# Edge counting in 128 groups of 256 edges with a 24-target span, against 64 groups of 512 with 40

## The chip, the cores and the metric

The kernel runs on one core of a Trainium2 chip. A core has a tensor engine (PE), a vector engine (DVE), a scalar engine (ACT), GpSimd (POOL) and a sync engine (SP), each with its own instruction stream; they wait for each other on semaphores. The metric is device time in microseconds (us) of one execution, and the median of several runs is compared.

## The reference, cut to what matters

Four graph layers, each followed by a residual and a normalisation, work on 1024 nodes of 512 features and 32768 edges, sorted by target. Everything the layers need of the graph comes from one table: how many edges lead from source s to target t.

```
x, src, dst: 1024x512 float32, 32768 int32, 32768 int32 (dst is sorted)
edge_index = stack([src, dst])
layer 0: adj.set(1) both ways, + eye, degree-normalised, adj @ (x @ weight) + bias
layer 1: three graph convolutions: segment_sum(xw[src] * norm, dst) + b
layer 2: q, k, v; attention masked by adj = zeros(N, N).at[src, dst].set(1)
layer 3: two graph convolutions, a relu between them
after each: x = layernorm(x + layer)
```

## The kernel before

The whole kernel is one block with a program written by hand for each engine. It has a counting stage and then the layers. The counting stage builds `count`, a table of 1024 sources by 1024 targets in SBUF, out of the sorted edge list.

The edges are cut into G groups of GE = CPG * 128. In each group the targets lie close together, and a window of WIN targets from the group's smallest one takes them all, if the group's span is under WIN. If the widest group's span is not, the stage is run again for the next WIN targets (a "round"; `rounds` is computed on the chip from the widest span). For one group there are CPG chunks of 128 edges, one edge per partition. Each chunk takes two one-hot matrices: `hot_lo`, 128 wide, the source modulo 128, and `hot_key`, KEYS = 8 * WIN wide, a key made of the source's block of 128 and the target's place in the window. One bf16 matmul per chunk multiplies the two (L479), and the CPG chunks are summed in one PSUM bank. DVE then adds the bank to the window of `count` (L950).

The engines share this work as follows.

- DVE makes every `hot_key` (L936) and the `hot_lo` of the first BY_DVE chunks (L934) of group g+1, and then waits for the matmuls of group g and adds its window (L950). The target address comes from a register; eight registers are loaded at once, for BODY = 8 groups (L941).
- ACT makes the other `hot_lo` in two steps, since it has no comparison: the absolute difference into `apart`, one instruction per chunk (L788), then, after a wait for them, one relu over all of them into `hot_lo` (L792). It may start group g when the matmuls of group g-2 are done, since `hot_lo` and the PSUM banks 0 and 1 are used in turn. Behind that stand the copies of folding results from PSUM (L782 and neighbours), 512 columns each.
- PE waits for the add of group g-2 and for each one-hot, does the CPG matmuls, and then does its share of other work that doesn't need the graph: the "folding". That is a list of 48 units of 4 pieces each (transposes of x and of weights L419 and L423, products L431, L454, L458, L461, bias rows L436 and L449). A credit decides how many pieces stand behind a group: it grows by SHARE per group, and a piece costs 1024 of it for a 512-column product, 128 for a transpose and 256 for a piece of the small bias unit.

```
        for g in range(-1, G):
            m = n
            while credit > 0 and m < 4 * (NU - 1):
                credit -= weight_of(m)
                m += 1
            pieces[g] = (n, m)
            n = m
            credit = min(credit, 0) + SHARE
```

What is left of the list follows behind the last group; then come the transposes of the links (L521), the last unit, and layer 0 (L544). Each 1024-credit piece is one fp32 product, which the trace records as two matmuls.

POOL adds a bias to `xs` in eight instructions (L352) as soon as the small bias unit is out. That falls into the counting stage.

Of the kernel before, what the change touches and what calls it, by code (L numbers as in the profile page):

```python
# [28 lines left out]
NEG = -1000000.0  # L29
EXACT = 4096  # L30
FAR = 8192.0
CPG = 4
WIN = 40
BY_DVE = 2
EARLY = 24 * 128
SHARE = 1450
BODY = 8
HALF = 4

# [1 line left out]
def gnn_kernel(nc, x, src, dst, w0, b0, w1, b1, w2, b2, w3, b3, wq, bq, wk, bk, wv, bv, v1, c1, v2, c2, out):  # L41
# [3 lines left out]
    FB = D // P  # L45
    G = E // (CPG * P)
    GE = CPG * P
    ROUNDS = (N + WIN - 1) // WIN
    KEYS = NB * WIN
    SCALE = float(D) ** -0.5  # L50
    assert D == 512 and NB == 2 * HALF and G % BODY == 0 and KEYS <= 512 and G <= P

    with ExitStack() as ctx:
        place = [(nc.sbuf_base + 63) // 64 * 64]

        def region(size):

            start = place[0]
            place[0] += (size + 31) // 32 * 32
            assert place[0] <= nc.sbuf_usable_end  # L60
            return start

        def at(name, start, shape, dt):
            return nc.alloc_sbuf_tensor_at(name, shape, dt, offset=start)

        def sb(name, shape, dt):
            size = {F32: 4, F32R: 4, I32: 4, BF16: 2, I16: 2, U16: 2}[dt]
            for n in shape[1:]:
                size *= n
            return at(name, region(size), shape, dt)  # L70
# [5 lines left out]
        adj = sb("adj", [P, NB, N], F32R)  # L76
        count = sb("count", [P, NB, N + WIN], U16)
        xs = sb("xs", [P, NB, D], F32)
# [38 lines left out]
        key_rows = at("key_rows", r3 + 2 * W + 8192, [G, 3, GE], F32)  # L117
        keyed = at("keyed", r3 + 2 * W, [P, 3, CPG * G], F32)
        apart = at("apart", r3 + 2 * W + 8192, [P, 2, CPG - BY_DVE, P], BF16)
        link = at("link", r3 + 2 * W, [P, NB, N], BF16)  # L120
# [8 lines left out]
        r4 = region(W)  # L129
        hot_lo = at("hot_lo", r4, [P, 2 * CPG, P], BF16)  # L130
        hot_key = at("hot_key", r4 + 2 * CPG * P * 2, [P, 2 * CPG, KEYS], BF16)
        wv_sb = at("wv_sb", r4, [P, FB, D], F32)
# [125 lines left out]
        for g in range(-1, G):  # L258
# [5 lines left out]
            n = m  # L264
            credit = min(credit, 0) + SHARE
        ALONG = n
# [56 lines left out]
        def _(pool):  # L323
            chain = [0]

            def then(ins):
# [8 lines left out]
            nc.gpsimd.tensor_copy(identb[:], ident[:])  # L335
            nc.gpsimd.iota(span_at[:], pattern=[[WIN, ROUNDS]], base=0, channel_multiplier=0,
                           allow_small_or_imprecise_dtypes=True)
# [68 lines left out]
        def _(pe):  # L406
# [78 lines left out]
            for g in range(G):  # L485
                pe.wait_ge(win_added, g + 1)
                for c in range(CPG):
                    pe.wait_ge(hot_set, CPG * g + c + 1)
                    if c == BY_DVE:
                        pe.wait_ge(act_hot_set, g + 1)  # L490
# [7 lines left out]
            with pe.If(rounds > 1):  # L498
                with pe.Fori(1, rounds) as r:
                    with pe.Fori(0, G // BODY) as q:  # L500
                        for n in range(BODY):
                            pe.wait_ge(win_added, r * G + q * BODY + (n + 1))
                            for c in range(CPG):
                                pe.wait_ge(hot_set, (r * G + q * BODY) * CPG + (n * CPG + c + 1))
                                if c == BY_DVE:
                                    pe.wait_ge(act_hot_set, r * G + q * BODY + (n + 1))
# [254 lines left out]
        def _(act):  # L761
# [23 lines left out]
            def low_one_hots(g, slot, before):  # L785

                for c in range(BY_DVE, CPG):
                    ins = nc.scalar.activation(apart[:, slot, c - BY_DVE, :], col_lo[:], ACT.Abs, scale=-1.0,  # L788
                                               bias=edge_key[:, 0, bass.ds(g + c * G, 1)])
                ins.then_inc(apart_set, 1)  # L790
                act.wait_ge(apart_set, before + 1)
                nc.scalar.activation(hot_lo[:, slot * CPG + BY_DVE:(slot + 1) * CPG, :], apart[:, slot], ACT.Relu,  # L792
                                     scale=-1.0, bias=ones[:, 0:1]).then_inc(act_hot_set, 1)
# [95 lines left out]
        def _(dve):  # L889
# [20 lines left out]
            V.tensor_copy(key_rows[:, 0, :], bits[:, 0, :])  # L910
            V.tensor_scalar(key_rows[:, 1, :], bits[:, 1, :], float(WIN), None, ALU.mult)
            V.tensor_scalar(key_rows[:, 2, :], edge_rows[:, 0, :], group_lim[:, 0:1], None,
# [33 lines left out]
            def add_window(at_dst, seen, slot):  # L946

                dve.wait_ge(win_summed, seen + 1)
                dve.wait_ge(win_added, seen + 2)
                V.tensor_tensor(count[:, :, bass.ds(at_dst, WIN)],  # L950
                                bank[:, slot, 0:KEYS].rearrange("p (h d) -> p h d", h=NB),
# [251 lines left out]
```

## Time and profile before

| | us |
|---|---|
| median of 3 runs | 622.41 |
| lowest and highest run | 619.67, 624.84 |
| span of the profiled execution, first to last instruction | 620.4 |
| counting stage, first one-hot (ACT) to the end of the last window add | 14.4 to 144.7 |
| PE busy in the span | 593.8 |
| DVE busy in the span | 300.0 |
| ACT busy in the span | 180.1 |

The profiled execution has no time of its own in the list beside its span; the span lies between the lowest and the median run. Busy times are shares of engines, and an engine that is not on the chain that ends last may be idle at no cost. A matmul's duration in the trace includes its way through the array, so the step from one start to the next is the better measure of what it costs.

### The profile page before, as it was taken

The page shows a single profiled execution, that of the slowest core. Times are in us where ns is not written, and L with a number is a line of the kernel's source. Part 1 is how long each engine was busy: PE and PEld are TensorE (multiplying, and loading weights), DVE is VectorE, ACT ScalarE, POOL GpSimd, SP SyncE. Part 2 cuts the span into 40 slices and gives each one's busy share as a digit, 9 for nine tenths or more (in the row PEclk, how much of TensorE's full clock was granted, in tenths as well). Part 3 has the DMA queues.
Part 4 walks back from the last instruction along what each step waited for, and adds up shares of the span by engine and source line. Part 5 has one row for each costly group of instructions (what it writes and reads, how often), then busy time and mean ns, then how long its engine had stood idle before and what let it go on. Part 6 is the DMA issues. An engine that isn't in the chain of part 4 may idle for free.

```text
span 620.4 us, 6559 instructions
## 1 busy us (share of the span) xinstructions
PE 593.8 (96%) x2153; PEld 351.9 (57%) x2153; DVE 300.0 (48%) x818; ACT 180.1 (29%) x363; POOL 108.8 (18%) x121
## 2 busy tenths in 40 slices
PE   3997899999997999999999999999999999999996
PEld 3554365454665557888874544444444478548742
DVE  6989977895734710343459110323333550251055
ACT  2787467783610230121100301211112311221100
POOL 3003200000822530000026000222222161000012
PEclk9999798999998999999999999999999999999999
DMA  8500003002000000000004000000000000000012
GB/s 297 195 1 1 0 1 137 0 2 69 2 0 2 0 3 0 1 0 1 0 6 147 0 1 0 0 1 0 1 0 0 2 1 1 0 0 1 0 52 85
DMA packets 7903, 15.65 MB, mean 25 GB/s; under 512 B 432, under 2 KB 448, under 8 KB 7872
## 3 DMA queue, kind: packets, MB, share of 16 engines
q1 hardware_dynamic: 7872, 15.21, 7.0%
q8 instruction: 22, 0.36, 0.2%
q14 instruction: 9, 0.07, 0.0%
HBM read 13.12 MB, written 2.10 MB: 25 GB/s over the span
## 4 chain that ended last, share of the span: by engine, by line
PE 90%; DVE 4%; ACT 2%; issue 2%; DMA 0%; POOL 0%; POOLq 0%; SPq 0%; DVEq 0%; ACTq 0%
PE bank L544 17%; PE bank L597 17%; PE bank L561 10%; PE bank L706 9%; PE bank L726 9%; PE bank L479 6%; PE bank L694 4%; PE bank L454 4%; PE bank L458 2%; PE bank L461 2%; PE bank L431 2%; PE bank L449 2%; PE bank L716 1%; PE bank L624 1%; DVE hot_key L936 1%
## 5 line engine op out<-in xcount | busy, mean ns | idle before, releaser
L370 POOL TENSOR_TENSOR rstd<-veps,mhalf 128x1 f32<-128x1 f32 x32 | 23.6, 737 | 299.4 <-DVE veps L1009 292.4
L936 DVE TENSOR_SCALAR hot_key<-col_key,keyed 128x320 bf16<-128x320 int16 x256 | 70.5, 317 | 0.0
L706 PE MATMUL bank<-xt,tt 128*128 128x512 f32 x128 | 56.1, 592 | 0.0
L726 PE MATMUL bank<-vv,probt 128*128 128x512 f32 x128 | 56.1, 592 | 0.0
L597 PE MATMUL bank<-v_sb,gt 128*128 128x512 f32 x128 | 55.3, 592 | 0.0
L479 PE MATMUL bank<-hot_key,hot_lo 128*128 128x320 bf16 x256 | 48.5, 309 | 4.6 <-DVE hot_key L936 4.5
L479 PEld LDWEIGHTS bank<-hot_key,hot_lo 128*128 128x128 bf16 x256 | 25.7, 100 | 47.2 <-issue 21.8
L788 ACT ACTIVATE apart<-col_lo,edge_key 128x128 bf16<-128x128 int16 x128 | 44.4, 396 | 26.8 <-PE bank L479 26.6
L561 PE MATMUL bank<-adj,y_hi 128*128 128x512 f32 x128 | 51.8, 405 | 0.0
L544 PE MATMUL bank<-ya_hi,adj 128*128 128x512 f32 x128 | 50.9, 398 | 0.0
L544 PE MATMUL bank<-ya_lo,adj 128*128 128x512 f32 x128 | 50.5, 395 | 0.0
L561 PE MATMUL bank<-adj,y_lo 128*128 128x512 f32 x128 | 50.2, 392 | 0.0
L1016 DVE SCALAR_TENSOR_TENSOR xs<-bank,dinv,xs 128x512 f32<-128x512 f32 x24 | 17.9, 747 | 53.9 <-PE bank L597 38.4
L597 PEld LDWEIGHTS bank<-v_sb,gt 128*128 128x128 f32 x128 | 24.3, 190 | 29.8 <-issue 29.2
L726 PEld LDWEIGHTS bank<-vv,probt 128*128 128x128 f32 x128 | 24.2, 190 | 29.6 <-issue 29.6
L706 PEld LDWEIGHTS bank<-xt,tt 128*128 128x128 f32 x128 | 23.9, 190 | 27.7 <-issue 27.7
L950 DVE TENSOR_TENSOR count<-bank,count 128x320 f32 x64 | 31.2, 487 | 14.6 <-PE bank L479 14.5
L1116 DVE SCALAR_TENSOR_TENSOR score<-bank,rr,mask 128x1024 f32<-128x1024 f32 x8 | 10.3, 1284 | 55.5 <-PE bank L706 55.5
L934 DVE TENSOR_SCALAR hot_lo<-col_lo,edge_key 128x128 bf16<-128x128 int16 x128 | 34.4, 268 | 3.4 <-issue 3.3
L454 PE MATMUL bank<-w_sb,x0t 128*128 128x512 f32 x64 | 31.7, 597 | 2.0 <-ACT x0t L769 1.7
L792 ACT ACTIVATE hot_lo<-apart,ones 128x256 bf16<-128x256 bf16 x64 | 32.5, 508 | 2.1
L544 PE MATMUL bank<-ya_hi,sym 128*128 128x512 f32 x64 | 28.0, 438 | 4.5 <-DVE flags L1057 3.7
(172 smaller groups left out, 894.5 us busy)
## 6 DMA issues: line engine op xcount, KB each, us to landing
w_sb<-in_L_gnn_W_dram SPq DMA_DIRECT2D x3, 1024.0 KB, 7.7
xs<-in_x_dram SPq DMA_DIRECT2D x2, 1024.0 KB, 8.2
v_sb<-in_L_gnn_W_dram SPq DMA_DIRECT2D x2, 1024.0 KB, 6.8
out_dram<-xs SPq DMA_DIRECT2D x8, 256.0 KB, 2.0
w_sb<-in_L_gnn_weight_dram SPq DMA_DIRECT2D x1, 1024.0 KB, 8.5
wq_sb<-in_L_gnn_Wq_dram SPq DMA_DIRECT2D x1, 1024.0 KB, 12.5
wk_sb<-in_L_gnn_Wk_dram SPq DMA_DIRECT2D x1, 1024.0 KB, 13.9
wv_sb<-in_L_gnn_Wv_dram SPq DMA_DIRECT2D x1, 1024.0 KB, 6.4
```

The source lines that it names most:

```text
L454: mm = pe.matmul(to, x0t[:, k, rows], w0_sb[:, k, :], start=first, stop=last)
L479: return pe.matmul(bank[:, at_bank, 0:KEYS], hot_lo[:, at_hot, :], hot_key[:, at_hot, :], start=c == 0, stop=c == CPG - 1)
L544: mm = pe.matmul(to, m[:, k, j * P:(j + 1) * P], y[part][:, k, :], start=k == 0 and part == 0 and m is mat, stop=k == NB - 1 and part == 1 ...
L561: mm = pe.matmul(to, y[part][:, k, f * P:(f + 1) * P], m[:, k, half], start=k == 0 and part == 0 and m is mat, stop=k == NB - 1 and part = ...
L597: mm = pe.matmul(bank[:, HALF * (s % 2) + b, :], g[:, k, j * P:(j + 1) * P], w[:, k, :], start=k == 0, stop=k == FB - 1)
L706: mm = pe.matmul(bank[:, 2 * (i % 2) + c, :], tt[:, k, i * P:(i + 1) * P], xt[:, k, c * D:(c + 1) * D], start=k == 0, stop=k == FB - 1)
L726: mm = pe.matmul(bank[:, 6 + i % 2, :], probt[:, i % 2, j, :], vv[:, j, :], start=j == 0, stop=j == NB - 1)
L788: ins = nc.scalar.activation(apart[:, slot, c - BY_DVE, :], col_lo[:], ACT.Abs, scale=-1.0, bias=edge_key[:, 0, bass.ds(g + c * G, 1)])
L792: nc.scalar.activation(hot_lo[:, slot * CPG + BY_DVE:(slot + 1) * CPG, :], apart[:, slot], ACT.Relu, scale=-1.0, bias=ones[:, 0:1]).then_i ...
L934: V.tensor_scalar(hot_lo[:, slot * CPG + c, :], col_lo[:], edge_key[:, 0, bass.ds(g + c * G, 1)], None, ALU.is_equal)
L936: V.tensor_scalar(hot_key[:, slot * CPG + c, :], col_key[:], keyed[:, 0, bass.ds(g + c * G, 1)], None, ALU.is_equal).then_inc(hot_set, 1)
L950: V.tensor_tensor(count[:, :, bass.ds(at_dst, WIN)], bank[:, slot, 0:KEYS].rearrange("p (h d) -> p h d", h=NB), count[:, :, bass.ds(at_dst ...
```

## The change

Four numbers change, and through them the sizes and counts. G goes from 64 to 128, GE from 512 to 256, KEYS from 320 to 192. A group now has two chunks, one low one-hot by DVE and one by ACT. The credit per group is half. No other line changes.

```diff
-CPG = 4
-WIN = 40
-BY_DVE = 2
+CPG = 2
+WIN = 24
+BY_DVE = 1
 EARLY = 24 * 128
-SHARE = 1450
+SHARE = 725
 BODY = 8
 HALF = 4
```

On PE, in the first part of the counting stage, the matmuls of one or more groups (L479) stand between products of the folding (L454: the rows of x by the weight of layer 0). Before:

```order
L479 MATMUL bank<-hot_key,hot_lo 128x320 x4
L454 MATMUL bank<-w_sb,x0t 128x512
L479 MATMUL bank<-hot_key,hot_lo 128x320 x4
L454 MATMUL bank<-w_sb,x0t 128x512 x2
L479 MATMUL bank<-hot_key,hot_lo 128x320 x4
```

After the change:

```order
L479 MATMUL bank<-hot_key,hot_lo 128x192 x2
L454 MATMUL bank<-w_sb,x0t 128x512
L479 MATMUL bank<-hot_key,hot_lo 128x192 x4
L454 MATMUL bank<-w_sb,x0t 128x512
L479 MATMUL bank<-hot_key,hot_lo 128x192 x2
L454 MATMUL bank<-w_sb,x0t 128x512
L479 MATMUL bank<-hot_key,hot_lo 128x192 x2
```

A group is four matmuls before and two after; where "x4" stands after the change, two groups follow each other with no folding between them. There were one or two folding products behind each group, and there is now one or none.

On ACT, at the start of the stage, before:

```order
L788 ACTIVATE apart<-col_lo,edge_key 128x128 x2
L792 ACTIVATE hot_lo<-apart,ones 128x256
L788 ACTIVATE apart<-col_lo,edge_key 128x128 x2
L792 ACTIVATE hot_lo<-apart,ones 128x256
L782 COPY xw<-bank 128x512
```

After the change:

```order
L788 ACTIVATE apart<-col_lo,edge_key 128x128
L792 ACTIVATE hot_lo<-apart,ones 128x128
L788 ACTIVATE apart<-col_lo,edge_key 128x128
L792 ACTIVATE hot_lo<-apart,ones 128x128
L782 COPY xw<-bank 128x512
```

Each group's pair on ACT has become one difference and one relu of half the width, and there are twice as many groups.

On DVE, one group of the loop before (with the register instructions between the operations):

```order
L934 TENSOR_SCALAR hot_lo<-col_lo,edge_key 128x128
L936 REGISTER_ALU
L936 TENSOR_SCALAR hot_key<-col_key,keyed 128x320
L934 ISA
L934 TENSOR_SCALAR hot_lo<-col_lo,edge_key 128x128
L936 REGISTER_ALU
L936 TENSOR_SCALAR hot_key<-col_key,keyed 128x320
L936 ISA
L936 TENSOR_SCALAR hot_key<-col_key,keyed 128x320
L936 ISA
L936 TENSOR_SCALAR hot_key<-col_key,keyed 128x320
```

After the change, with the add that follows:

```order
L934 TENSOR_SCALAR hot_lo<-col_lo,edge_key 128x128
L936 REGISTER_ALU
L936 TENSOR_SCALAR hot_key<-col_key,keyed 128x192
L936 ISA
L936 TENSOR_SCALAR hot_key<-col_key,keyed 128x192
L948 ISA
L949 REGISTER_ALU
L950 ISA
L950 TENSOR_TENSOR count<-bank,count 128x8x24
```

A window add now stands behind three one-hot instructions where it stood behind six.

## Rows read from the trace of the kernel before

**Rows 1.** The page: the span, and PE's busy tenths in 40 slices.
```profile
span 620.4 us, 6559 instructions
PE   3997899999997999999999999999999999999996
```

**Rows 2.** The chain that ended last, in order of time (start, us, what).
```profile
60.23 3.71 DVE hot_key L936 x3
...
144.00 7.74 PE bank L461 x18
152.40 1.51 PE bank L521 x24
```

**Rows 3.** The timeline, 22.0 to 26.2 (start, us, engine, line, operation, idle before).
```profile
22.04 0.71 PE L479 MATMUL bank<-hot_key,hot_lo 128*128 128x320 bf16 x4
...
22.59 1.02 PE L454 MATMUL bank<-w_sb,x0t 128*128 128x512 f32 x2
22.79 0.69 ACT L788 ACTIVATE apart<-col_lo,edge_key 128x128 bf16<-128x128 int16 x2 [0.82 <-PE bank L479]
22.98 0.49 DVE L950 TENSOR_TENSOR count<-bank,count 128x320 f32 x1 [0.43 <-PE bank L479]
...
23.39 0.24 DVE L934 TENSOR_SCALAR hot_lo<-col_lo,edge_key 128x128 bf16<-128x128 int16 x1
23.45 0.71 PE L479 MATMUL bank<-hot_key,hot_lo 128*128 128x320 bf16 x4
...
23.51 0.51 ACT L792 ACTIVATE hot_lo<-apart,ones 128x256 bf16<-128x256 bf16 x1
23.55 0.30 DVE L936 TENSOR_SCALAR hot_key<-col_key,keyed 128x320 bf16<-128x320 int16 x1
23.76 0.25 DVE L934 TENSOR_SCALAR hot_lo<-col_lo,edge_key 128x128 bf16<-128x128 int16 x1
...
23.99 1.88 PE L454 MATMUL bank<-w_sb,x0t 128*128 128x512 f32 x4
...
24.56 0.48 DVE L950 TENSOR_TENSOR count<-bank,count 128x320 f32 x1
...
24.91 0.51 ACT L792 ACTIVATE hot_lo<-apart,ones 128x256 bf16<-128x256 bf16 x1
24.96 0.24 DVE L934 TENSOR_SCALAR hot_lo<-col_lo,edge_key 128x128 bf16<-128x128 int16 x1
...
25.33 0.57 ACT L782 COPY xw<-bank 128x512 f32<-128x512 f32 x1
...
25.70 0.71 PE L479 MATMUL bank<-hot_key,hot_lo 128*128 128x320 bf16 x4
```

**Rows 4.** Waits, 15 to 145 (us in total, times, longest).
```profile
ACT apart L788 <- PE bank L479: 26.6, 33, 4.9
...
DVE count L950 <- PE bank L479: 14.5, 21, 4.8
...
PE bank L479 <- DVE hot_key L936: 4.5, 5, 2.1
```

**Rows 5.** One line each: ACT's differences, DVE's register loads (min/median/max ns).
```profile
L788 ACT ACTIVATE apart<-col_lo,edge_key x128: 384/400/433, 14.4 to 140.9; 128x128 bf16<-128x128 int16 x128
```

```profile
L941 DVEq TENSOR_LOAD <-base_at x8: 594/599/633, 15.5 to 130.2; - x8
```

**Rows 6.** The timeline: a stretch of transposes, and DVE behind a register load.
```profile
30.74 0.26 DVE L934 TENSOR_SCALAR hot_lo<-col_lo,edge_key 128x128 bf16<-128x128 int16 x1 [0.46 <-issue]
...
48.50 1.47 PE L423 MATMUL bank<-ident,wq_sb 128*128 128x128 f32 x12
```

**Rows 7.** Windows of 3 us (busy time and count by engine, PE's granted clock).
```profile
51.00:54.00 3.00, 2.35 (x17) 1.83 (x17) 3.00 (x15) 2.97 (x9) 0.00 (x0) 1.00 0.02 5
...
60.00:63.00 3.00, 0.53 (x2) 0.19 (x2) 3.00 (x4) 0.00 (x0) 3.00 (x4) 1.00 0.00 0
63.00:66.00 3.00, 2.09 (x4) 0.58 (x3) 3.00 (x4) 1.20 (x3) 3.00 (x3) 0.55 0.00 0
66.00:69.00 3.00, 2.62 (x7) 1.15 (x7) 3.00 (x13) 1.13 (x3) 0.28 (x1) 0.50 0.00 0
```

## The prediction

> **What bounds the kernel now.** I read the page first. PE is busy nine tenths or more in most slices, the counting stage included [rows 1], so the question is whether PE itself or its partners set the pace there. The chain of waits answers it for the end of the stage: PE runs through its leftover folding (7.74 us) and goes straight on to the link transposes [rows 2]. The leftover folding hides the last window add and what DVE does to the links, so the rest of the kernel starts when PE's list is done, and the stage is worth what PE spends in it, work and waits. The list behind it isn't touched, nor is anything after 152 us.
>
> Then I read the timeline group by group, from one start to the next, since matmul durations overlap [rows 3]. PE starts a group at 22.04, 23.45 and 25.70. The first lasts 1.41 us: 0.54 for the four counting matmuls (23.45 to 23.99) and 0.86 for one product of the folding. The second has two products and lasts 2.25. Neither has a gap: with the sum 0.54 + 0.86 n the group is over when PE's own work is. DVE needs less for a group: its adds start at 22.98 and 24.56, a period of 1.58 us, and it is DVE that waits for PE (14.5 us in all); ACT waits for PE as well (26.6 us); PE waits for one-hots only 4.5 us [rows 4]. These 4.5 us are in one place, where POOL adds its biases and each DVE one-hot takes over 1.2 us (three in 3.71) [rows 2]. So PE binds, and its partners have slack.
>
> **Does the narrower window suffice?** From the reference's inputs, the widest of the 128 groups spans 17 targets, less than 24. There is one round, as before (widest of the 64: 32, under 40).
>
> **PE's counting matmuls (a gain).** 64 groups x 0.54 = 34.6 us. Four matmuls of 320 columns in 0.54 is 0.135 each; by columns, 192 take 0.081. 128 groups x 0.16 = 20.5 us. Gain 14.1 us at the clock of the rows. The folding is the same list, and because the credit per edge is the same, it ends at the same place of the list: no change, and the 7.74 us leftover stays.
>
> **What DVE needs per group.** From starts [rows 3]: `hot_lo` 0.16 (23.39 to 23.55), a 320-wide `hot_key` 0.21 (23.55 to 23.76), the 320-wide add 0.40 (24.56 to 24.96). That is 2 x 0.16 + 4 x 0.21 + 0.40 = 1.56. Widths 128 and 320 differ by 0.05, so a 192-wide key takes about 0.175. The add has no row at another width. Ends: 0.24, if all of it goes with the columns, and 0.40, if none does. I take 0.27 (0.13 us less for 128 columns fewer), nearer the first, because the one-hots show a fixed part of some 0.12 and no more. Then 0.16 + 2 x 0.175 + 0.27 = 0.78 per group of half the size: the same time per edge, hence no gain on DVE. The registers are loaded every eight groups, so 16 times and not 8; a load takes 0.6 [rows 5] and shows as 0.46 of idle time before the next one-hot [rows 6], that is 0.06 more per group: 0.84.
>
> **What ACT needs per group.** The two differences take 0.69, the relu starts 0.03 after them (22.79 to 23.51), and it holds the engine for 0.42 (24.91 to 25.33) [rows 3]; a single difference takes 0.40 [rows 5]. That is 1.14 per group, 73 us in all. After the change one difference stands before its wait: 0.40 + 0.04, and nothing overlaps it. A 128-wide relu holds the engine for about 0.30: no row shows it, but the second of two 128-wide differences adds 0.29 (0.69 less 0.40), and the 256-wide relu's 0.42 is the upper end. So 0.74 per group, 128 x 0.74 = 95 us: 22 us more for the same edges. Some 42 copies at 0.50 (0.57 less the overlap of 0.09) stand between: 21 us, or 0.16 per group.
>
> A rule of the Trainium skill bears on both engines: "VectorE: DVE Perf Modes", section on the TRN2 errata, states a fixed cost per instruction, 58 cycles plus the width over the mode's factor on VectorE and 224 cycles on ScalarE. By it a 192-wide one-hot would be about 0.11 us and DVE's group near 0.65; the rows have 0.16 for the narrowest one, so the row is used. If the rule's figure held in this loop, the forecast would be about 3 us lower.
>
> **The hand-offs (a loss).** PE needs 0.16 + 0.86 n, with n one or none. Averaged over the credit (725 of 1024) that is 0.77, beside 0.84 for DVE and 0.90 for ACT. What were 1.75, 1.62 and 1.5, with PE the slowest, are now nearly equal, with PE the fastest; PE must wait. Where it does follows from the order of instructions. Of the 127 groups with a successor, 75 have one product behind them, 32 have none, 20 have transposes or the small bias unit.
>
> - One product: PE has 1.02 us of its own, more than its partners. Wait about 0.03. 75 x 0.03 = 2 us; ends 0 and 0.2 each (15 us), the latter if PE meets a partner that is behind.
> - None: PE has only 0.16, and the two buffers carry it one group ahead at most. Over a typical run of three groups (product, product, none) PE has 2 x 1.02 + 0.16 = 2.20, DVE 2.5, ACT 2.5 (3 x 0.74 and half a copy). So the empty group can't take less than about 0.47. If it waits for a full period of DVE, it takes 0.78. The add can start 0.4 us after the last matmul's issue (the matmuls of 22.04 end at 22.75, the add starts at 22.98) [rows 3], and that delay now stands in a group half as long. I take 0.65, in the middle: wait 0.49, 32 x 0.49 = 16 us; ends 10 and 20.
> - Transposes: six or so behind a group, at 0.12 [rows 6], are 0.16 + 0.72 = 0.88 for PE; in nearly each such group a 512-wide copy falls due on ACT, which then needs 0.74 + 0.50 = 1.24. The copies lag a little and are partly caught up. Wait 0.2 each, 4 us; ends 0 and 7.
>
> Sum of waits 22 us, less the gain of 14: **+8 us**. With all low ends it is -4, with all high ends +28, which would need every partner late in every group. POOL's stretch stays as it is: its eight instructions block DVE's one-hots for the same time, and the one-hots per edge are as many as before (six for 512 edges, three for 256), so PE loses the same there. DVE's setup ahead of the loop gets shorter in the 64-partition steps, but PE waits there for x, not for it: nothing.
>
> **The clock.** PE's granted clock is 1.00 up to 63 us and then 0.55 and 0.50, 1.2 GHz, after PE had been busy for 0.53 of 3 us in POOL's stretch; with 2.35 of 3 it stayed at 1.00, 2.4 GHz [rows 7]. After the change PE would be busy some 83% of the stage, in gaps under 0.6 us, nearer to the second row. So I count no further loss, and keep one as a rival.
>
> **Rivals.**
>
> 1. *The engines' slack suffices*: each group costs what the slowest engine needs and no more; the empty groups take 0.47, the transposes nothing. For it: PE, DVE and ACT wait for each other through two buffers and the groups without a product are evenly spread. Against: three engines with nearly the same load rarely mesh. Sum -14 + 10 + 2 to 4: about 0, 622 us.
> 2. *PE stays the slowest*: the one-hot instructions turn out shorter at half width (a relu near 0.2, an add near 0.2), and DVE and ACT fall under 0.7 per group. The waits shrink to some 5 us in all. Then the columns saved are gained: 622.4 - 9 = 613 us. It decides at a partner's load of 0.77 per group, PE's own. Against it: the differences' 0.40 and the keys' 0.16 are at 128 columns already and can't shrink.
> 3. *The clock falls as well*: PE's micro-gaps bring it to 1.2 GHz in further stretches. A product then takes 1.72 and the partners have to wait. With two or three more such stretches of 7 us as in 63 to 70 [rows 7], each costing 3 to 4 us, +16 to +18 in all: 639 us. For it: half as much cover at each gap, and the transposes' stretches, in which PE waits most. Against it: the row at 2.35 of 3 us. The Trainium skill has this as a rule, in "TensorE: Matmul & The Clock Gate", section "A second HAM failure mode: psum-queue depth-cycling": frequent micro-idles between groups of matmuls that cycle through banks make the clock oscillate. No row of before shows that.
> 4. *A second round* would add a whole stage, over 100 us. The inputs exclude it.
>
> **How the numbers follow.** The sum is made against the span of 620.4; the median is 2.0 above it, and the difference is carried over: 622.4 + 8 = 630.5 (own range 626 to 636). Chances: forecast 0.50, rival 1 0.20, rival 2 0.08, rival 3 0.22. The runs shown spread over 5 us, so 1%, 6.2 us, is about what a measurement can tell from no change. Slower by over 1% (above 628.6): 0.42 of the forecast's 0.50 and rival 3, 0.64. Within 1%: the rest of the forecast and nearly all of rival 1, 0.27. Faster: rival 2 and a little of rival 1, 0.09. A range from 620 to 642 leaves out rival 2, the lower part of rival 1 and the far end of rival 3, less than 0.2 together.
>
> **What the profile after would show.** PE's steps with one product near 1.02 to 1.05, the empty ones near 0.65: under 0.5 speaks for rival 1 or 2, over 0.8 for a dearer hand-off. The steps from DVE add to one-hot, 0.27, and from ACT's relu to the next instruction, 0.30, are the two sizes not seen. The last window add should end near 152.5 and not at 144.7, the leftover folding follow it unchanged, and PE's wait for one-hots of both kinds rise from 4.5 to over 20 us. A granted clock under 1.00 outside the two stretches of before would be rival 3. The prediction is wrong above all if ACT or DVE run their narrow instructions faster than their 128-wide ones of before.

## The result, and the profile after

The changed kernel takes 635.14 us at the median (634.49 to 636.41, 4 runs), the kernel before 622.41. The ratio is 1.0224, with a 95% interval of 1.0193 to 1.0255: slower by 12.7 us by the medians and by 13.9 us by the ratio. The profiled execution has a span of 633.9 us, 13.5 more than before.

The page, span and PE by slices, to be read beside [rows 1]:

```profile
span 633.9 us, 6994 instructions
...
PE   4987689989999799999999999999999999999996
```

PE's digits have fallen to 6 to 9 in the first quarter, where almost all were 9. The first link transpose on the chain of waits shows where the time went. It stood at 152.40 [rows 2]:

```profile
157.47 6.29 PE bank L461 x14
163.78 0.59 ACT wfold L782
164.42 1.51 PE bank L521 x24
```

So 12.0 of the 13.5 us are in the counting stage. Most of the rest, 1.2 us, is at the first feature transposes (L624), 1.75 us on the chain before and 2.97 after: the 1.2 GHz stretch at PE's wait there lasts 6.8 us, where it lasted 3.4. The same place has either length in the runs below. In the counting stage the difference goes the other way: the 1.2 GHz stretch behind the bias unit lasts 3.4 us in this trace (98.6 to 102.0) and 6.8 in that of before (90.6 to 97.4). If such a stretch costs half its length, which is an estimate, that is up to 1.7 us in favour of the changed kernel, and at equal clock the stage has grown by up to 13.7 us.

Now the groups, in the timeline of the changed kernel at the place of [rows 3]:

```profile
21.81 0.36 DVE L950 TENSOR_TENSOR count<-bank,count 128x192 f32 x1 [0.27 <-PE bank L479]
22.05 0.40 ACT L792 ACTIVATE hot_lo<-apart,ones 128x128 bf16<-128x128 bf16 x1
22.09 0.24 DVE L934 TENSOR_SCALAR hot_lo<-col_lo,edge_key 128x128 bf16<-128x128 int16 x1
22.25 0.44 DVE L936 TENSOR_SCALAR hot_key<-col_key,keyed 128x192 bf16<-128x192 int16 x2
22.36 0.39 ACT L788 ACTIVATE apart<-col_lo,edge_key 128x128 bf16<-128x128 int16 x1
22.61 0.35 DVE L950 TENSOR_TENSOR count<-bank,count 128x192 f32 x1
22.70 0.33 PE L479 MATMUL bank<-hot_key,hot_lo 128*128 128x192 bf16 x2
...
22.90 1.10 PE L454 MATMUL bank<-w_sb,x0t 128*128 128x512 f32 x2
...
23.72 0.25 DVE L934 TENSOR_SCALAR hot_lo<-col_lo,edge_key 128x128 bf16<-128x128 int16 x1 [0.76 <-issue]
...
24.30 0.37 PE L479 MATMUL bank<-hot_key,hot_lo 128*128 128x192 bf16 x2 [0.29 <-DVE hot_key L936]
```

The add holds DVE for 0.28 (21.81 to 22.09), the relu holds ACT for 0.31 (22.05 to 22.36): the sizes that no row of before showed are as estimated. Then DVE loads eight registers, is idle for 0.76, its next one-hots come late, and PE, whose product began at 22.90 and has some 0.9 us of work in it, starts the next group only at 24.30: this group lasts 1.60 us. The waits of the stage, to be read beside [rows 4]:

```profile
ACT apart L788 <- PE bank L479: 19.0, 32, 2.2
PE bank L479 <- DVE hot_key L936: 14.6, 22, 2.2
...
DVE hot_lo L934 <- issue: 12.4, 16, 0.9
DVE count L950 <- PE bank L479: 12.0, 36, 2.1
PE bank L479 <- ACT hot_lo L792: 2.7, 5, 1.0
```

PE's wait for DVE has gone from 4.5 to 14.6 us, and DVE's idle time behind its 16 loads is 12.4, 0.77 each. Of the low one-hots of ACT PE waits only 2.7.

From the starts of each group's first matmul in the trace, and for the groups called quiet without POOL's stretch and the slow-clock stretch behind the bias unit:

| groups of the changed kernel | count (quiet) | forecast, us | mean | median |
|---|---|---|---|---|
| one product behind | 75 (65) | 1.05 | 1.22 | 1.18 |
| none behind | 32 (29) | 0.65 | 0.46 | 0.35 |

In the kernel before, the quiet groups with one product all took 1.40 and those with two 2.26 (median), PE's own work.

Two things in the trace say where the excess stands. The 12 quiet groups in whose course DVE loads its registers, so that the next group's one-hots come late, take 1.66 with a product and 1.15 without; the others take 1.15 and 0.38. And a product itself has become dearer: its second matmul starts 0.43 us after the first in the trace of before, and 0.46 or 0.50 in the changed kernel, the longer step in 15 of the 18 products just behind a wait of PE and in 22 of the 54 others. Over these 72, all outside the slow-clock stretches, it is 3.8 us. Why a product costs more behind a small group isn't shown.

### The profile page after: what moved, and what is told of

Its sections match the earlier page's. It is cut to its first block, busy times and chain, and to the rows that moved or that the text cites. A ratio compares the mean times of both kernels' runs of the same rounds, so it can differ in the third digit from the quotient of the medians.

```text
span 633.9 us, 6994 instructions
## 1 busy us (share of the span) xinstructions
PE 594.7 (94%) x2147; PEld 345.0 (54%) x2147; DVE 304.6 (48%) x882; ACT 201.2 (32%) x427; POOL 108.7 (17%) x121
## 4 chain that ended last, share of the span: by engine, by line
PE 79%; DVE 9%; issue 5%; ACT 4%; DVEq 2%; POOL 0%; DMA 0%; POOLq 0%; SPq 0%
PE bank L544 17%; PE bank L597 17%; PE bank L561 9%; PE bank L706 9%; PE bank L726 9%; PE bank L694 4%; DVE hot_key L936 3%; PE bank L454 3%; PE bank L479 2%; PE bank L461 2%; PE bank L449 2%; DVE hot_lo L934 2%; PE bank L624 1%; ACT hot_lo L792 1%; PE bank L716 1%
## 5 line engine op out<-in xcount | busy, mean ns | idle before, releaser
L479 PEld LDWEIGHTS bank<-hot_key,hot_lo 128*128 128x128 bf16 x256 | 25.0, 99 | 80.3 <-issue 51.3
L479 PE MATMUL bank<-hot_key,hot_lo 128*128 128x192 bf16 x256 | 46.1, 248 | 18.2 <-DVE hot_key L936 14.6
L936 DVE TENSOR_SCALAR hot_key<-col_key,keyed 128x192 bf16<-128x192 int16 x256 | 61.9, 284 | 0.1
L788 ACT ACTIVATE apart<-col_lo,edge_key 128x128 bf16<-128x128 int16 x128 | 50.7, 396 | 20.3 <-PE bank L479 19.0
L792 ACT ACTIVATE hot_lo<-apart,ones 128x128 bf16<-128x128 bf16 x128 | 51.4, 402 | 4.1
L950 DVE TENSOR_TENSOR count<-bank,count 128x192 f32 x128 | 45.5, 356 | 13.7 <-PE bank L479 12.0
L934 DVE TENSOR_SCALAR hot_lo<-col_lo,edge_key 128x128 bf16<-128x128 int16 x128 | 33.5, 262 | 12.4 <-issue 12.4
L454 PE MATMUL bank<-w_sb,x0t 128*128 128x512 f32 x64 | 34.6, 622 | 2.3 <-ACT x0t L769 2.3
```

The lines of the kernel that those rows point to most:

```text
L454: mm = pe.matmul(to, x0t[:, k, rows], w0_sb[:, k, :], start=first, stop=last)
L479: return pe.matmul(bank[:, at_bank, 0:KEYS], hot_lo[:, at_hot, :], hot_key[:, at_hot, :], start=c == 0, stop=c == CPG - 1)
L934: V.tensor_scalar(hot_lo[:, slot * CPG + c, :], col_lo[:], edge_key[:, 0, bass.ds(g + c * G, 1)], None, ALU.is_equal)
L936: V.tensor_scalar(hot_key[:, slot * CPG + c, :], col_key[:], keyed[:, 0, bass.ds(g + c * G, 1)], None, ALU.is_equal).then_inc(hot_set, 1)
L950: V.tensor_tensor(count[:, :, bass.ds(at_dst, WIN)], bank[:, slot, 0:KEYS].rearrange("p (h d) -> p h d", h=NB), count[:, :, bass.ds(at_dst ...
```

## The experiments

Each ratio is to runs of the kernel before on the same chip; the changed kernel is at 1.0224 on this scale, and 0.01 is 6.2 us. These intervals are 0.0013 to 0.003 to either side. The runs of the kernel before aren't all alike, even on one chip: 620.6 us and less where the granted clock was 0.986 or more, 621.8 and more where it was 0.984 or less. So a ratio also carries which of the two a chip's runs happened to show, and differences under some 2 us between runs on different chips aren't sure. "Links start" is the first L521 in the trace: 152.4 before, 164.4 after.

**Deeper buffers (e1_deep).** Four buffers of one-hots, four PSUM banks, DVE two groups ahead, and ACT's wait for a free buffer set back likewise. The main lines of the edit:

```diff
-        hot_lo = at("hot_lo", r4, [P, 2 * CPG, P], BF16)
+        hot_lo = at("hot_lo", r4, [P, SLOTS * CPG, P], BF16)
-                pe.wait_ge(win_added, g + 1)
+                pe.wait_ge(win_added, max(g + 3 - SLOTS, 2))
-                        one_hots(q * BODY + (n + 1), (n + 1) % 2)
+                        one_hots(q * BODY + (n + AHEAD), (n + AHEAD) % SLOTS)
```

> The changed kernel (635.1 us) with four buffers of one-hots and four PSUM banks where there are two, and DVE making its one-hots two groups ahead. No work is changed. Theory H (hand-offs: the groups cost more than the busiest engine needs because two buffers tie PE, ACT and DVE together): quiet groups fall from a mean near 0.98 us towards ACT's own 0.90, so 8 to 10 us come back, 625 to 627. Rival L (load: DVE or ACT alone sets the pace, its instructions plus the register loads are what a group costs): no more than 2 us come back, 633 to 635.

Measured: 626.92 us, ratio 1.0105 (1.0082 to 1.0128), links start at 155.6. 7.4 us of 13.9 come back by the ratio, 8.2 by the medians, and the links start 8.9 earlier with 1.2 GHz stretches of the same length. So H holds for the greater part, and L is out. The empty groups take 0.165 at the median and those with a product 1.05, PE's own; by the mean it is 0.29 and 1.21, so some groups still wait. What PE still waits for:

```profile
PE bank L481 <- DVE hot_key L938: 9.5, 16, 2.3
PE bank L481 <- ACT hot_lo L794: 5.2, 11, 1.0
```

**Sixteen registers at a load (e2_body16).**

```diff
-BODY = 8
+BODY = 16
```

> The changed kernel with the registers of the window targets loaded for 16 groups at once, so 8 loads and not 16. In the changed kernel DVE sat idle 12.4 us behind the 16 loads, 0.77 each. If the load sits on the path each time (theory: the register loads are a dearer term of the sum than the 0.46 taken from before), 8 x 0.6 to 0.8 = 5 to 6 us come back: 629 to 630. Rival: PE or ACT is behind anyway when the load comes, and at most 2 us come back, 633 or more.

Measured: 632.55 us, ratio 1.0198 (1.0174 to 1.0222). That is 1.6 us at the centre, within the intervals, and near the rival's figure; but the rival's reason isn't shown by it, since the edit didn't do what I meant. Half as many loads take nearly twice as long each, and DVE sits idle behind the 8 for 10.1 us where it was 12.4 behind 16. The line of the loads in this run (median 1101 ns; 599 for eight registers [rows 5]):

```profile
L941 DVEq TENSOR_LOAD <-base_at x8: 1096/1101/1133, 14.8 to 138.2; - x8
```

From these two durations the price is 0.06 us per register and 0.1 per load, an estimate, so it goes with the number of groups.

**ACT's difference ahead (e3_actpipe).** The main lines of the edit:

```diff
+            low_apart(0, 0)
             for g in range(G):
-                if g >= 2:
-                    act.wait_ge(win_summed, g - 1)
-                low_one_hots(g, g % 2, g)
+                if g + 1 < G:
+                    if g >= 3:
+                        act.wait_ge(act_hot_set, g - 2)
+                    low_apart(g + 1, (g + 1) % 4)
+                if g >= 2:
+                    act.wait_ge(win_summed, g - 1)
+                low_relu(g % 2, g % 4, g)
```

> The changed kernel with ACT's difference for group g+1 issued ahead of the relu of group g (four buffers for the differences), so that the relu's wait for its difference is covered. Occupancy per group by the rows of after: 0.74 falls to about 0.29 + 0.31 = 0.60, and the way from a freed buffer to the finished low one-hot from 0.84 to 0.41. If ACT's pair is what delays the groups (theory A), 6 to 12 us come back, 623 to 629. If DVE's one-hots and its loads are (rival D), under 2 us: 633 or more.

Measured: 631.71 us, ratio 1.0176 (1.0151 to 1.0201), links start at 162.0: 3.0 us. It lies between the two: ACT isn't the main delay while there are two buffers, but it isn't nothing. (In the traces the links start 2.4 us earlier.)

**The grouping alone (e4_win40).**

```diff
-WIN = 24
+WIN = 40
```

> One part of the change alone: 128 groups of 256, with the old window of 40 targets (320 columns). Per group PE then needs 0.27 for its matmuls and not 0.16, DVE 0.06 to 0.07 more for two wider keys and 0.13 more for the add. Theory: with partners as the pace, DVE's 0.20 more per group counts in full, 128 x 0.2 = 25 us: 660. Rival (PE's columns count, since it is PE that is on the chain): 128 x 0.107 = 14 us, 649. Against the kernel before it is the grouping alone, so the narrower window is worth the difference of this run to 635.

Measured: 642.68 us, ratio 1.0364 (1.0338 to 1.0391), links start at 172.1. The grouping alone costs 22.7 us, and the narrower window gives 8.7 back. Both figures for the latter were too high, and neither theory holds in full. The quiet groups with a product keep their 1.22 and only the empty ones grow, from 0.46 to 0.73: a group with a product had room for DVE's longer instructions, and an empty one hadn't, as I read it; no run separates the two.

**Deeper buffers and ACT ahead (e5_deep_act).** The two edits together.

> Both earlier edits together on the changed kernel: four buffers and banks, and ACT's differences issued ahead. With the buffers alone (ratio 1.0105 to the kernel before) ACT still keeps PE waiting 5.2 us, at the copies. If those waits are what is left besides DVE's loads, 3 to 5 us more come back: ratio 1.003 to 1.006. If DVE's own pace (its instructions and the register loads, some 0.86 us a group) is the limit now, less than 1.5 us: ratio 1.008 to 1.011.

Measured: 621.4 us, ratio 0.998 (0.9966 to 0.9994), links start at 150.1. With both edits the kernel is level with the one before: the whole loss has come back, 15.2 us by the ratio and 13.7 by the medians. How much of it the second edit adds to the first is less sure, since the two ran on different chips: 7.8 us by the ratios, 5.5 by the medians. In the trace the links start 5.5 us earlier than in e1_deep, of which up to 1.7 are the clock's: the stretch at 1.2 GHz behind POOL's adds lasts 3.4 us here and 6.8 in e1_deep. That leaves 3.8, inside the 3 to 5 expected. PE's wait for ACT's one-hots has fallen from 5.2 to 1.0 us, which is of that size:

```profile
PE bank L481 <- ACT hot_lo L797: 1.0, 2, 0.5
```

That ACT's pair was worth more with four buffers than its 3 us with two isn't shown.

**No register loads (e6_noload).** The output is not the reference's: all windows go to eight fixed places, and the add takes a fixed address with them. The step from an add to the next one-hot stays 0.27 us, so the address form changes nothing.

```diff
-                _, values = nc.values_load_multi_w_load_instructions(
-                    base_at[0:1, bass.ds(g, BODY)], engines=[mybir.EngineType.DVE], min_val=0, max_val=N,
-                    skip_runtime_bounds_check_because="the table's entries are clamped to [0, N] when it is written")
+                values = [n * P for n in range(BODY)]
-                V.tensor_tensor(count[:, :, bass.ds(at_dst, WIN)],
+                V.tensor_tensor(count[:, :, at_dst:at_dst + WIN],
```

> The changed kernel without the register loads: the windows go to eight fixed places of the count table, so the targets of the edges are left out of the placing; every count, add, one-hot and matmul stays. In the trace of the changed kernel a group at nearly every eighth place lasts 0.6 to 1.2 us longer. Theory: each of the 16 loads (0.60 us for 8 registers, over 1.1 for 16) falls on the path; without them 10 to 13 us come back, 622 to 625 where the changed kernel has 635. Rival: PE would wait for the hand-offs instead, and 4 us or less come back (631 or more).

Measured: 629.72 us, ratio 1.0116 (1.0098 to 1.0135), links start at 159.3. The loads are on the path: 6.7 us come back by the ratio (5.4 by the medians), between the theory's 10 to 13 and the rival's 4 at most. DVE now waits for PE in 47 groups and not 36, for 19.1 us and not 12.0, so part of the time taken away comes back as that wait.

```profile
DVE count L948 <- PE bank L479: 19.1, 47, 3.2
```

**A narrower window alone (e7_win34),** in the kernel before.

```diff
-WIN = 40
+WIN = 34
```

> The kernel before, 64 groups of 512, with a window of 34 targets (the widest group spans 32), 272 columns for 320. If PE's columns set the pace there (steps of 1.40 and 2.26 without a gap), 256 x 48 columns at 2.4 GHz = 5.1 us come off: ratio 0.992. If DVE or ACT would be next at once, less than half of it: 0.996 or more.

Measured: 616.9 us, ratio 0.9914 (0.9895 to 0.9932), links start at 146.1. The whole 5 us came. (In the traces the links start 6.3 us earlier, up to 1.7 of it from a shorter 1.2 GHz stretch behind the bias unit.) The timeline of PE shows a step of 1.32 with one product (1.40 before) and 2.18 with two (2.25), with no gap:

```profile
21.78 0.63 PE L479 MATMUL bank<-hot_key,hot_lo 128*128 128x272 bf16 x4
22.25 1.02 PE L454 MATMUL bank<-w_sb,x0t 128*128 128x512 f32 x2
23.10 0.63 PE L479 MATMUL bank<-hot_key,hot_lo 128*128 128x272 bf16 x4
23.57 1.88 PE L454 MATMUL bank<-w_sb,x0t 128*128 128x512 f32 x4
25.28 0.63 PE L479 MATMUL bank<-hot_key,hot_lo 128*128 128x272 bf16 x4
```

This version beats both kernels with one number, and is the best here that computes the reference.

**The partners' pace by itself (e8_nofold).**

```diff
-SHARE = 725
+SHARE = 0
```

> The changed kernel with no folding between the groups (a share of 0): all of it runs behind the last group. Not meant as an improvement; it shows what a group costs when PE has only its two matmuls. By DVE's rows (0.78 of instructions and a load of 0.6 to 0.76 every eight groups) 0.86 to 0.88 us per group; ACT alone would give 0.74. If the hand-off chain through two buffers is longer than that, 1.0 us or more. PE would be at 1.2 GHz here.

Measured: 695.36 us in its one run, PE at 1.2 GHz for 122.9 us. Only the group's period is of use. Its timeline, a group and the next behind a load:

```profile
65.33 0.48 PE L479 MATMUL bank<-hot_key,hot_lo 128*128 128x192 bf16 x2 [0.31 <-DVE hot_key L936]
...
66.12 0.48 PE L479 MATMUL bank<-hot_key,hot_lo 128*128 128x192 bf16 x2 [0.31 <-DVE hot_key L936]
...
67.27 0.25 DVE L934 TENSOR_SCALAR hot_lo<-col_lo,edge_key 128x128 bf16<-128x128 int16 x1 [0.85 <-issue]
...
67.85 0.48 PE L479 MATMUL bank<-hot_key,hot_lo 128*128 128x192 bf16 x2 [1.25 <-DVE hot_key L936]
...
68.73 0.48 PE L479 MATMUL bank<-hot_key,hot_lo 128*128 128x192 bf16 x2 [0.40 <-DVE hot_key L936]
```

A group takes 0.79 (median 0.786), which is DVE's 0.78 of instructions; the hand-offs add nothing to it. Behind a load it takes 1.73. The 127 steps sum up to 115.6 us, 0.91 each: (115.6 - 127 x 0.786) / 16 = 0.99 us per load on average, twice what I had counted.

**The share undone (e9_share1450).**

```diff
-SHARE = 725
+SHARE = 1450
```

> The changed kernel with one part undone: the folding share per group is 1450 again, so the folding is used up after some 65 of the 128 groups. Those have one or two products (0.16 + 1.22 on average = 1.38 us, PE's own), the 62 or so behind them have none and go at DVE's pace, 0.91 (the run without folding). Sum: 65 x 1.38 + 62 x 0.91 = 146 us where the changed kernel's groups took 141, and no folding is left to cover the last window add and the links, but 6.3 us of it no longer stands behind the stage either. Theory (pace of DVE where PE has nothing): near the changed kernel, -2 to +4 us: ratio 1.02 to 1.03. If the halved share were itself what costs the time, this would be back near the kernel before: 1.01 or less.

Measured: 658.32 us, ratio 1.0588 (1.0559 to 1.0618). The halved share isn't what costs the time; with the old one it would have been far worse. The time lies 18 us over the upper end of my own figure. The 58 empty groups do take 0.90 each, as in the run without folding. But the sum for the others left out POOL's stretch, the transposes and the slow clock (112 us and not 90), and PE's clock falls to 1.2 GHz once the folding is used up. PE was busy for 1.95 of 3 us and then 1.04 of 3 before that (126 to 132), and in it:

```profile
130.00:150.00 20.00, 10.34 (x44) 4.53 (x44) 17.94 (x89) 16.56 (x44) 0.00 (x0) 0.57 0.00 1
150.00:170.00 20.00, 10.23 (x44) 4.36 (x42) 17.43 (x87) 16.49 (x44) 0.00 (x0) 0.50 0.00 0
```

The clock stays at 0.50 for 54.6 us in this trace, into the first 24 link transposes, which take 4.25 us where they took 1.51.

**Everything ahead, window of 18 (e10_deep_act_win18).**

```diff
-WIN = 24
+WIN = 18
```

> The changed kernel with four buffers, ACT's differences ahead, and a window of 18 targets (the widest group spans 17), 144 columns for 192. With the buffers PE is mostly without a gap (steps 1.05 and 0.165 at the median), so 256 x 48 columns = 5.1 us of PE and 128 x 0.05 of DVE's add come off. If PE or DVE sets the pace either way: ratio 0.990 to 0.992 where the same with 24 had 0.998. If DVE's one-hots and register loads are what is left, which hardly shrink: 0.995 to 0.998.

Measured: 619.55 us, ratio 0.996 (0.9945 to 0.9975). Within the second figure: 256 x 48 columns less bring 1 us and not the 5 of e7_win34. PE is no longer what paces the stage here. The shortest group with a product has itself fallen by only 0.02, from 1.05 to 1.03, where the columns are worth 0.04. Further narrowing doesn't bring the small groups level with the large ones.

**Everything ahead, no loads (e11_deep_act_noload).** The output again leaves the targets out.

> The changed kernel with four buffers and ACT's differences ahead, and without the register loads (windows at eight fixed places, so the edges' targets are left out of the placing). With two buffers the loads cost 6.7 us. If the deeper buffers already hide a load (1.0 us, a little more than one group), it gives nothing: ratio 0.997 to 0.999. If DVE's pace with the loads (0.91 a group) is still above PE's 0.77, DVE falls behind in any case and the loads count: 0.990 to 0.994.

Measured: 615.69 us, ratio 0.9897 (0.9881 to 0.9914), 5.2 us under e5_deep_act. Deeper buffers don't hide the loads: they take DVE's own time, as e8_nofold shows. The empty groups, outside POOL's stretch and those at 1.2 GHz, now all take 0.165.

## Why the prediction came out as it did

The direction and the reason held: the columns saved on PE were given back, and more, as waits. The forecast was 630.5 (its sum gives 630.3 to 630.4), the result 635.1, inside the range of 620 to 642 and near the end of the forecast's own range. That it came so near is in part luck, since the two main waits were wrong in opposite ways: by the quiet means the groups with a product waited 15 us and not 2, the empty ones 10 us and not 16.

- *What bounds before.* PE's own work in the counting stage. e7_win34 shows it: 5.1 us of columns taken away, 5 us gained.
- *The narrower window suffices.* One round; the stage isn't repeated.
- *PE's matmuls, -14.1.* The shortest empty group takes 0.16, as forecast. A product costs more than 0.86: 0.94 behind a wait (26.22 to 27.16 in the timeline), and 0.89 at the least. The shortest group with a product is 1.05 and not 1.02, which alone is some 2 us over 75 groups, and 3.8 us with the longer steps inside the products counted in full.
- *DVE per group.* 0.78 of instructions was right (0.786). **The register loads were the mis-sized term.** I took the 0.46 of one load in the kernel before. The waits of before, in the window of [rows 4], have six idle stretches behind loads, and they are uneven:

```profile
DVE hot_lo L934 <- issue: 3.3, 6, 0.7
```

Three of them are 0.74 (at 45.46, 82.85 and 117.53) and three 0.46, 0.37 and 0.29. The long ones are those where DVE had waited for PE just before the add; there the load starts at the add's end (0.49 after its start), in the short ones already 0.1 to 0.2 after its start. So a wait for PE doesn't hide a load; why it starts earlier in the other three isn't shown. In the changed kernel 14 of the 16 are like the long ones, 0.69 to 0.88. With PE nowhere in the way the price is 0.99. So DVE's pace is 0.91 per group and not 0.84, 9 us more over 128 groups; what of the loads reaches the end is the 6.7 us of e6_noload, and I had let through some 2 us of them, the 0.03 at each group with a product. The difference is as large as that between forecast and result, but the dearer products and the two wrong waits stand beside it, and no run divides the 4.6 us among them.
- *ACT per group.* 0.74 was right (0.31 for the relu, 0.42 to 0.43 for the difference and its wait). ACT was not the slowest partner, as I had it with the copies at 0.90 beside DVE's 0.84: with its loads DVE was level with it at 0.91, and PE's waits ended on DVE for 14.6 us, POOL's stretch included, and on ACT for 2.7.
- *The hand-offs.* Near in sum, wrong in place. The empty groups took 0.46 and not 0.65, and the groups with a product 1.22 and not 1.05; a group in whose course DVE loads its registers takes 0.5 to 0.8 us more than the others of its kind. The 16 groups with transposes alone took 1.15 at the mean, where 1.08 was counted. For 94 quiet groups the forecast gives 87 us and the trace 93. That two buffers are what turns near-equal loads into waits is shown: 7.4 us come back by four buffers, 15.2 with ACT's pair ahead as well.
- *The clock.* No further loss, as forecast: outside the stretches behind POOL's adds, the bias unit and the first feature transposes, all known from before, the changed kernel's stage is at 1.00. Three of its windows of 3 us in which PE was less busy, to be read beside [rows 7]:

```profile
81.00:84.00 3.00, 2.01 (x11) 0.97 (x10) 2.33 (x12) 2.15 (x6) 0.00 (x0) 1.00 0.00 0
...
108.00:111.00 3.00, 2.14 (x9) 0.77 (x7) 2.17 (x11) 2.94 (x9) 0.00 (x0) 1.00 0.97 364
...
132.00:135.00 3.00, 2.07 (x9) 0.96 (x8) 2.12 (x12) 2.33 (x7) 0.00 (x0) 1.00 0.00 0
```

What the Trainium skill says in "TensorE: Matmul & The Clock Gate", in its section on depth-cycling, of a clock that goes up and down with micro-idles between groups isn't seen in these windows. Nor is it what e9_share1450 shows: there the clock falls once and stays at 1.2 GHz for 54.6 us.
- *Fixed costs.* The Trainium skill's errata rule in "VectorE: DVE Perf Modes" gives (120 + 192) cycles, 0.325 us as an estimate, for the add out of PSUM, and 0.65 for DVE's whole group; the trace has 0.28 and 0.786. The same table's 224 cycles and 128 columns on ScalarE, 0.293 us as an estimate, are near the relu's 0.31.
- *The rivals.* Rival 1 (the slack suffices) had the empty groups right, 0.47 beside 0.46, and those with a product wrong, 1.02 to 1.05 beside 1.22; so an empty group under 0.5, which I had named as a sign for rival 1 or 2, was none. Rival 2 (PE stays slowest) needed DVE and ACT under PE's 0.77, and DVE has 0.91. Rival 3 needed further stretches at 1.2 GHz in the stage, and there are none. Of the other signs, the last window add was to end near 152.5 and ended at 156.8, and PE's wait for one-hots was to pass 20 us and came to 17.3.

What stays open: how much more ACT's pair is worth with four buffers than with two, which the clock's varying stretches hide with one trace per kernel; and why a product's two matmuls stand further apart behind a small group. POOL's stretch, in which a DVE one-hot takes over 1.2 us, stands in every version but e8_nofold, and moving it wasn't tried.

## What to carry to other kernels

Cutting a pipelined unit of work in two is free only for what scales with its size: here the columns on PE, while per group a register, a wait and a half-filled instruction stay. Before halving, add up each partner's time per unit, with the register loads at the price that most of their rows show and not the cheapest, and compare it with the engine that has the work. Here PE had 0.77 beside 0.90 and 0.91, and more buffers were due as well. A window that is as narrow as the data allow gave its saving in columns without any of this, as long as PE set the pace (e7_win34); where it didn't, it gave 1 us (e10_deep_act_win18).

## What the runs showed of the hardware

- A load of registers from SBUF on DVE's queue takes 0.60 us for eight and 1.10 for sixteen, and takes 0.99 us out of the engine's period when it alone sets the pace. Fewer, larger loads save little: 1.6 us by halving their number.
- Without folding, PE was busy half the time in matmuls of 192 columns and stayed at 1.2 GHz for 122.9 us. The same groups with folding between them, PE busy for 67 to 71% of the three windows of 3 us above, kept 2.4 GHz.
- The 1.2 GHz stretches behind one and the same wait lasted 3.4 us in some traces and 6.8 in others, by estimate up to 1.7 us of time. Executions of one kernel differ in granted clock as well: the kernel before took 619.1 us at a mean granted clock of 0.989 and 624.9 at 0.978. In a comparison at the 1% level this matters as much as a small edit.
- The two matmuls of an fp32 product of 512 columns started 0.43 us apart behind a group of four matmuls of 320 columns, and 0.46 or 0.50 apart behind one of two matmuls of 192.
